# Rounding weights to FP4 beside an attention: |q| on ScalarE, a maximum on VectorE, scales for two chunks at once, four buffers

## What is computed

```python
def fp4_quant_dequant(x):                        # blocks of 16 along the last dim
    scale = jnp.max(jnp.abs(xb), axis=-1, keepdims=True) / 6.0
    scale = jnp.maximum(scale, jnp.float32(1e-12))
    xn = xb / scale
    idx = jnp.searchsorted(_MID, jnp.abs(xn))    # _MID  0.25 0.75 1.25 1.75 2.5 3.5 5
    q = _GRID[idx] * jnp.sign(xn) * scale        # _GRID 0 .5 1 1.5 2 3 4 6

def fp4_linear(x, w):
    xq, wq = fp4_quant_dequant(x), fp4_quant_dequant(w)
    return jnp.einsum('bsk,nk->bsn', xq, wq)

gate, y = fp4_linear(x, w_gate), fp4_linear(x, w_up)      # w: 1408 x 512
h = jax.nn.silu(gate) * y
out = fp4_linear(h, w_down)
```

## Time and profile before

| | |
|---|---|
| median of 3 runs (lowest to highest) | 1689.22 us (1686.55 to 1689.85) |
| the profiled execution | 1689.68 us, its span 1687.9 us |
| busy in the span | PE 1471.6 (87%), PEld 1060.0 (63%), DVE 773.1 (46%), ACT 466.4 (28%), POOL 557.9 (33%) |
| the rounding of the gate and up weights | 227 to 341 us |
| the block that holds it | ends at 347.2 us, the next one starts at 348.4 us |

### The profile page before, as it was taken

How to read it: one execution, slowest core, us unless ns; L and a number is a source line. 1 busy time by engine, 2 the same in 40 slices (tenths; PEclk the granted TensorE clock), 3 DMA queues, 4 the chain that set the end, 5 groups by cost and what they waited for, 6 DMA issues and landing times. The chain is left out here.

```text
span 1687.9 us, 26535 instructions
## 1 busy us (share of the span) xinstructions
PE 1471.6 (87%) x11120; PEld 1060.0 (63%) x11120; DVE 773.1 (46%) x1333; ACT 466.4 (28%) x772; POOL 557.9 (33%) x315
## 2 busy tenths in 40 slices
PE   8788977477988999999999999999998896936796
PEld 3556755243444778778787787788776673415573
DVE  2455279989435341332322323222232315978913
ACT  0323301031111115243242433324243431303302
POOL 6102057656323032122122122231232324617701
PEclk9779975788998999999999999999999998967997
DMA  5300030010101411111111111111012016003000
GB/s 233 149 1 1 0 137 1 0 69 0 75 0 64 147 51 57 52 34 53 39 42 51 39 48 42 38 52 57 30 42 78 22 57 256 0 0 119 1 0 25
DMA packets 50101, 91.29 MB, mean 54 GB/s; under 512 B 28600, under 2 KB 41664, under 8 KB 46912
## 3 DMA queue, kind: packets, MB, share of 16 engines
q1 hardware_dynamic: 49984, 89.60, 15.1%
HBM read 79.89 MB, written 9.70 MB: 53 GB/s over the span
## 5 line engine op out<-in xcount | busy, mean ns | idle before, releaser
L1074 POOL TENSOR_TENSOR ctx_hi<-ctx_raw,one 128x1536 fp32r<-128x1536 f32 (+1 forms) x36 | 102.9, 2858 | 617.5 <-DMA ctx_raw<-in_ctx 426.0
L1328 DVE TENSOR_TENSOR V<-PS,vbias 128x512 f32<-128x512 f32 (+1 forms) x104 | 71.9, 691 | 338.0 <-PE PS L1114 337.8
L1256 ACT COPY ET<-PS 128x512 f32<-128x512 f32 (+1 forms) x224 | 129.6, 585 | 299.1 <-PE PS L1170 295.4
L1359 DVE TENSOR_SCALAR_CACHE_REDUCE E<-PS 128x384 f32<-128x384 f32 (+1 forms) x256 | 131.8, 571 | 159.6 <-PE PS L1147 159.0
L1170 PE MATMUL PS<-ident,E 128*128 128x128 f32 (+1 forms) x832 | 127.3, 278 | 8.8 <-ACT ET L1256 8.8
L1077 POOL TENSOR_TENSOR ctx_raw_r<-ctx_raw,ctx_hi 128x1536 fp32r<-128x1536 f32 (+1 forms) x36 | 131.2, 3644 | 2.8
L1114 PE MATMUL PS<-ctx_raw_r,wk_hi 128*128 128x384 f32 (+1 forms) x512 | 128.6, 355 | 0.0
L1114 PE MATMUL PS<-wv_lo,ctx_hi 128*128 128x512 f32 (+1 forms) x416 | 125.9, 405 | 0.0
L1114 PE MATMUL PS<-ctx_hi,wk_hi 128*128 128x384 f32 (+1 forms) x512 | 122.9, 361 | 2.5 <-POOL ctx_raw_r L1077 2.5
L1263 ACT ACTIVATE E<-E,peak 128x1601 f32<-128x1601 f32 x64 | 103.5, 1623 | 64.8 <-DVE peak L1364 64.8
L1114 PE MATMUL PS<-wv_hi,ctx_hi 128*128 128x512 f32 (+1 forms) x416 | 120.5, 411 | 0.8 <-issue 0.8
(11 more groups left out here) (283 smaller groups left out, 2383.3 us busy)
## 6 DMA issues: line engine op xcount, KB each, us to landing
ctx_raw<-in_ctx SPq DMA_DIRECT2D x27, 768.0 KB, 4.4
ctx_raw<-in_ctx_first SPq DMA_DIRECT2D x9, 900.0 KB, 4.6
rel_scr<-rel_out SPq DMA_DIRECT2D x8, 640.0 KB, 3.8
fwk<-in_fwk SPq DMA_DIRECT2D x1, 4096.0 KB, 25.4
fwv<-in_fwv SPq DMA_DIRECT2D x1, 4096.0 KB, 12.7
corr<-rel_scr SPq DMA_DIRECT2D x64, 48.0 KB
p_scr<-E SPq DMA_DIRECT2D x16, 192.0 KB, 2.3
near<-p_scr SPq DMA_DIRECT2D x64, 48.0 KB
```

Of the source, the lines that this page charges most:

```text
L1074: nc.gpsimd.tensor_tensor(ctx_hi[r][:, :, 0:n], ctx_raw[r][:, :, 0:n], one[:].unsqueeze(1).broadcast_to([P, KC, n]), ALU.mult).then_inc(S[ ...
L1256: nc.scalar.copy(ET[0:n, j % ET_RING, :], src[0:n, :]).then_inc(S["et_out"], 1)
L1328: v.tensor_tensor(V[0:rows, at % V_RING, :], bank(4 + NUMBER[unit] % 2)[0:rows, :], vbias[0:rows, :], ALU.add).then_inc(S["v_out"], 1)
L1359: v.tensor_scalar(E[:, p, k0:k0 + n], bank(r)[:, 0:n], 1.0, None, ALU.mult, ALU.max, accum_out=tops[:, p, c:c + 1]).then_inc(S["s_out"], 1)
```

## The change

`WeightRounding` no longer uses `Fp4` (which `fp4_layer` still does). It works in pairs of chunks. VectorE takes two block maxima, and makes scale, reciprocal and factor for both in one instruction each, of 88 numbers per partition. ScalarE makes |q| times GRID = 2^22 + 1 (`scalar`), VectorE takes the maximum of that and GRID (`floor`) for the pair before, and GpSimd adds and subtracts that number as before. Mask (L581) and magic number (L582) are gone. GpSimd joins chunks 0 to 7, VectorE 8 to 15 (`join_by_vector`). q and grid have four buffers, the scales three pairs. ScalarE's 16 instructions are placed in the attention's program: two after each copy of the context, two after the exponential of t = 2 and t = 3 and in the same place at the last tile, two at the end.

```diff
@@ small_attention, vector
                 other(2)
+            if beside:
+                beside.finish(dve)
@@ small_attention, scalar
             for t in range(NT):
                 if t + 1 < NT:
                     exponentials(t + 1)
+                if beside and t >= 1:
+                    beside.scalar(act, 2)
                 act.wait_ge(pt_ps, t + 1)
...
                 act.wait_ge(o_ps, t + 1)
                 nc.scalar.copy(oT[...]).then_inc(o_out, 1)
+                if beside:
+                    beside.scalar(act, 2)
+            if beside:
+                beside.scalar(act, 2)
@@ WeightRounding
-    BY_POOL = CHUNKS - 5
+    BY_POOL = CHUNKS // 2
+    STAGES = 4
+    GRID = 2.0 ** 22 + 1.0
...
     def vector(self, dve, ch, count):
-        for n in range(self.started, min(self.started + count, self.CHUNKS)):
-            if n % (self.CHUNKS // 2) == 0:
-                dve.wait_ge(self.s.loaded["wg" if n == 0 else "wu"], 16)
-            self.fp4.divide(dve, ch, n, self.chunk(n))
-            self.started = n + 1
-            for k in range(self.CHUNKS):
-                if k >= self.BY_POOL and (k + 2 == n or (n == self.CHUNKS - 1 and k + 2 > n)):
-                    self.fp4.join(dve, self.nc.vector, k, self.chunk(k))
+        v = self.nc.vector
+        for n in range(self.started, min(self.started + count, self.CHUNKS), 2):
...
+            if n >= 2 * len(self.scale):
+                for k in range(2):
+                    self.wait_joined(dve, n + k - 2 * len(self.scale))
+            for k in range(2):
+                ch.add(v.tensor_reduce(self.scale_of(n + k), self.chunk(n + k), AX.X, ALU.max, apply_absolute_value=True))
+            ch.sync()
+            sc, inv = self.scale[n // 2 % len(self.scale)][:], self.inverse[:]
+            ch.link(v.tensor_scalar(sc, sc, float(np.float32(1 / 6)), 1e-12, ALU.mult, ALU.max))
+            ch.link(v.reciprocal(inv, sc))
+            ch.link(v.tensor_scalar(inv, inv, 1.0 - 2.0 ** -23, None, ALU.mult))
+            self.floor(dve, n)
+            self.join_by_vector(dve, n - 2)
+            for k in range(2):
+                if n + k >= self.STAGES:
+                    self.wait_joined(dve, n + k - self.STAGES)
+                v.tensor_tensor(blocks(self.q[(n + k) % self.STAGES][:]), self.chunk(n + k),
+                                inv[:, k].unsqueeze(2).broadcast_to([P, self.WIDTH // BLOCK, BLOCK]), ALU.mult).then_inc(self.divided, 1)
+            self.started = n + 2
+
+    def floor(self, dve, end):
+        for n in range(self.floored, end):
+            grid = self.grid[n % self.STAGES][:]
+            dve.wait_ge(self.sized, n + 1)
+            self.nc.vector.tensor_scalar(grid, grid, self.GRID, None, ALU.max).then_inc(self.ready, 1)
+        self.floored = max(self.floored, end)
+
+    def join_by_vector(self, dve, end):
+        for n in range(self.joined, end):
+            dve.wait_ge(self.rounded, 2 * n + 2)
+            self.join(self.nc.vector, n).then_inc(self.joined_dve, 1)
+        self.joined = max(self.joined, end)
+
+    def finish(self, dve):
+        self.floor(dve, self.CHUNKS)
+        self.join_by_vector(dve, self.CHUNKS)
+
+    def scalar(self, act, count):
+        for n in range(self.measured, min(self.measured + count, self.CHUNKS)):
+            act.wait_ge(self.divided, n + 1)
+            self.nc.scalar.activation(self.grid[n % self.STAGES][:], self.q[n % self.STAGES][:], ACT.Abs,
+                                      scale=self.GRID).then_inc(self.sized, 1)
+            self.measured = n + 1
...
     def pool(self, pool):
         for n in range(self.CHUNKS):
-            self.fp4.round(pool, n, self.WIDTH)
+            q, grid = self.q[n % self.STAGES][:], self.grid[n % self.STAGES][:]
+            pool.wait_ge(self.ready, n + 1)
+            self.nc.gpsimd.tensor_tensor(q, q, grid, ALU.add).then_inc(self.rounded, 1)
+            pool.wait_ge(self.rounded, 2 * n + 1)
+            self.nc.gpsimd.tensor_tensor(q, q, grid, ALU.subtract).then_inc(self.rounded, 1)
             if n < self.BY_POOL:
-                self.fp4.join(pool, self.nc.gpsimd, n, self.chunk(n))
+                pool.wait_ge(self.rounded, 2 * n + 2)
+                self.join(self.nc.gpsimd, n).then_inc(self.done, 1)
```

More of the change, by code:

```diff
@@ L608 @@
     CHUNKS = 2 * IC * D // WIDTH
-    BY_POOL = CHUNKS - 5
+    BY_POOL = CHUNKS // 2
+    STAGES = 4
+    GRID = 2.0 ** 22 + 1.0
     def __init__(self, nc, sem, region, s):
-        self.nc, self.s, self.fp4, self.started = nc, s, Fp4(nc, sem, region, "fp4w", self.WIDTH, 3), 0
+        self.nc, self.s, self.started, self.measured, self.floored, self.joined = nc, s, 0, 0, 0, self.BY_POOL
+        nb = self.WIDTH // BLOCK
+        self.q = [region.tensor(f"fp4w_q{r}", [P, self.WIDTH]) for r in range(self.STAGES)]
+        self.grid = [region.tensor(f"fp4w_grid{r}", [P, self.WIDTH]) for r in range(self.STAGES)]
+        self.scale = [region.tensor(f"fp4w_scale{r}", [P, 2, nb]) for r in range(self.STAGES // 2 + 1)]
+        self.inverse = region.tensor("fp4w_inverse", [P, 2, nb])
+        self.divided, self.sized, self.ready, self.rounded, self.done = (
+            sem("fp4w_" + n) for n in ("divided", "sized", "ready", "rounded", "done"))
+        self.joined_dve = sem("fp4w_joined_dve")
     def chunk(self, n):
@@ L617, in chunk, with scale_of, wait_joined @@
         return blocks(w[:, n * self.WIDTH:(n + 1) * self.WIDTH])
+    def scale_of(self, n):
+        return self.scale[n // 2 % len(self.scale)][:, n % 2]
+    def wait_joined(self, eng, n):
+        if n < self.BY_POOL:
+            eng.wait_ge(self.done, n + 1)
+        else:
+            eng.wait_ge(self.joined_dve, n - self.BY_POOL + 1)
     def vector(self, dve, ch, count):
-        for n in range(self.started, min(self.started + count, self.CHUNKS)):
+        v = self.nc.vector
+        for n in range(self.started, min(self.started + count, self.CHUNKS), 2):
@@ L631, in pool, with join @@
+    def join(self, ops, n):
+        return ops.tensor_tensor(self.chunk(n), blocks(self.q[n % self.STAGES][:]),
+                                 self.scale_of(n).unsqueeze(2).broadcast_to([P, self.WIDTH // BLOCK, BLOCK]), ALU.mult)
     def pool(self, pool):
         for n in range(self.CHUNKS):
-            self.fp4.round(pool, n, self.WIDTH)
+            q, grid = self.q[n % self.STAGES][:], self.grid[n % self.STAGES][:]
[3 more added lines that the diff above has]
+            self.nc.gpsimd.tensor_tensor(q, q, grid, ALU.subtract).then_inc(self.rounded, 1)
```

## The result

The changed kernel takes 1678.11 us (median of 4 runs, 1674.96 to 1680.29) against 1689.45 us; the ratio is 0.9934, 95% interval 0.9919 to 0.9949. It is faster by 0.7%, 11.3 us, where 7.7 us were forecast; the time lies inside the stated range. The profiled execution took 1677.72 us, its span 1675.9 us.

What follows compares the result with a forecast made beforehand. VectorE was taken to bound the edited block. Its stretches sum to 119.1 us against 128.0; with 1.1 us added for the layout's shortfall, it ends 7.7 us earlier: 1689.22 becomes 1681.5 us, range 1676 to 1688.5.

Steps and rivals of the forecast that it cites:

- What bounds: Second small attention, rounding of gate and up weights: VectorE limits the block; its gains move everything behind one for one.
- The turns: In the rounding, VectorE's port-using instructions and GpSimd's exclude each other and alternate; a VectorE product costs 2.27 us per turn.
- A removed instruction gives back its own part: VectorE in the rounding: removal saves the instruction's own time; its wait moves to the next one needing a turn.
- The count of 28 us: Rival counting VectorE's removed time alone, waits shrinking with the instructions: 28 us saved, 1661 us; chance 0.08 with anything near.
- The stretches: Block laid out from weigh(t) to weigh(t+1) for t=0 to 3, then the end: sum 119.1 us against 128.0.
- The second maximum: Second pair at t=0: VectorE's second maximum of |q| and GRID comes behind GpSimd's add, 2.1 us.
- |q| on ScalarE: 16 instructions of 0.76 us each; GpSimd's first add waits behind the context copy until 235.2, costing VectorE nothing.
- rival (3): Slower: ScalarE reloads its function table between Exp and Abs, five times in the block; 1686 or 1691 us; chance 0.06.
- near 340: Sign of a right forecast: the second small attention block ends near 340 us instead of 347.
- the blocks behind shift as a whole; I allow 1 us either way: Blocks after the changed one move by its gain, with 1 us allowed either way.

Runs made afterwards that it cites:

- without GpSimd's turns: GpSimd's three instructions a chunk cut to 16 of 704 numbers, in both kernels: stretch 87.94 us before, 78.03 after; single executions of 1659.21 and 1646.11 us.
- the mask: Changed kernel with exponent mask and magic number back on VectorE, ScalarE making nothing: stretch 121.05 us for 112.40; kernel 1690.66 us, ratio 1.0004 to the kernel before.
- the scales: Changed kernel with scale, reciprocal and factor made for each chunk by itself: stretch 117.50 us for 112.40; kernel 1685.53 us, ratio 0.9987 to the kernel before.
- The second comparison: Changed kernel, unedited, run again beside the kernel before on another run's chip: stretch 112.35 us; kernel 1681.05 us over 7 runs for 1688.79, ratio 0.9954.

## Why the prediction was right, and where its size was off

- **What bounds.** VectorE, and a quarter of the old stretch is its waiting for turns. Shown: without GpSimd's turns VectorE's busy time falls from 112.06 to 81.47 us, and the old stretch from 119.95 to 87.94.
- **The turns.** A product 2.27 us from turn to turn: two divisions took 4.66, a join 2.17 on average. A removed instruction gives back its own part: shown by the mask (8.7 us for instructions of 8.4 us) and the scales (5.1 us for 4.1 and their gaps). The joins don't follow it: two fewer on VectorE gave 3.0 us for 1.8 of their own, eight fewer cost 0.7, because those turns go to GpSimd. The count of 28 us was wrong for the reason given; the 20 us by which the divisions grew and the 10 of the joins ate it.
- **The stretches.** 22.2, 25, 26.4, 30 and 15.6 us plus 1.1 were laid out; 21.52, 26.43, 26.42, 30.03 and 16.46 were measured. The second is 1.4 off: the softmax product met a running GpSimd instruction there too, 2.50 us for 1.22, which I had charged to the third stretch alone. The row, which is the same again in the third stretch:

```profile
240.16 2.50 DVE L381 TENSOR_TENSOR XT<-XN,a_sm 128x1024 f32<-128x1024 f32 x1
```

  The second maximum, which I had behind GpSimd's add in the first stretch, got its turn ahead of it, and both divisions waited instead. That was one turn fewer: maxima and divisions took 5.6 us where 6.9 were laid out. A longer wait for the scores, 8.5 us until the first block maximum for 8.0, took some of it back. The prediction's addition is off too. The parts as it lists them, rounded as they are, make 22.35, 25.3, 26.7, 30.1 and 15.6, together 120.1 and not 119.1, so they give 6.8 us and not 7.7.
- **|q| on ScalarE.** 0.79 us for an estimated 0.76; GpSimd's first add at 233.63 in a block that began some 1.7 us earlier, so 235.3 on the old clock for 235.2. The wait that it adds to VectorE is 0.4 us, once. The reloads of rival (3) didn't come: the first table load behind the start of the span is still that of the SiLU in the next block:

```profile
356.23 1.28 ACT L854 ACT_TABLE_LOAD   x1
```

  Here "ScalarE: Activation LUTs" of the Trainium skill, section "Table sets: the hidden batching unit", which lists abs in the set of exp, is borne out: 16 Abs among the Exp without a load.
- **The block as a whole** got shorter by 7.1 us over the stretches as I laid them out (128.0 to 120.86), and by 7.55 from the first block maximum on, where I had 7.7. It ends at 337.97 us, 339.6 on the old clock, where "near 340" was expected. That it comes so close is partly luck: the turn too many in the first stretch and the product missed in the second, 1.3 us each, cancel.
- **The step that failed** is "the blocks behind shift as a whole; I allow 1 us either way". What lies outside the stretch was 4.5 us shorter in the profiled execution (1563.50 for 1567.95), 1.7 of it ahead of the change. Over 14 profiled executions it moved by 6 us with the same work in it, so a single comparison can carry 3 to 4 us that aren't the change's. The second comparison gave 7.7 us, the stretch's own gain: its median is 2.9 us above the first, and its profiled execution took 1340.83 us behind the stretch for the 1340.71 of the kernel before. The changed kernel's two values for the outside, 1563.50 and 1564.05, are still the lowest of the fourteen. The second is low by its part ahead of the change (223.22), which the change can't have shortened. So nothing here shows that any of the 11.3 us beyond the 7.55 belongs to the change, and a share of 1 to 3 us is not excluded. What sets TensorE's time for the same matmuls in the last blocks no run separated; its granted clock there is 0.85 in both rows.

## What to carry over

- When two engines exclude each other at a port, read an instruction's duration as work plus waiting, and price an edit by laying the new order out in turns. An instruction taken away gave back its own work here (mask, scales); the wait moves to the next one that needs the port.
- Then order matters as well as count. An instruction that needs no port costs nothing between two that do (4.65 us with it, 4.66 without), though only part of that reached the end: 3.0 us for moving 14 block maxima. Moving work to the other engine pays only while that one runs dry: of 8, 10 and 16 joins on GpSimd, 10 was best.
- Judge such a change by the stretch that it touches, where two executions agree to 0.05 us, and only then by the whole, where they don't agree to 3 (two executions of one code, 1565.46 and 1568.39 us outside the stretch).

## What the runs showed of the hardware

- VectorE and GpSimd take turns one instruction each. In the changed kernel's block 28 of VectorE's instructions and 34 of GpSimd's that use the port were held by more than 0.1 us, taking the shortest of each form as its own time, and neither engine got two in a row while the other waited; nor did it in the block of any other trace kept here. The two divisions in 4.66 us are one such place. "SBUF — State Buffer" of the Trainium skill, section "Who interferes with whom", calls the shared ports an exclusive lock that is held for the whole instruction, and the traces agree: the division issued at 248.77 waits out GpSimd's add until 250.39.
- A tensor_scalar of 88 numbers per partition waits for a running GpSimd instruction to its end just as one of 704 does: 1.54 us (L660, a row of the changed kernel's timeline, below) for 0.21, behind GpSimd's instruction that ends at 258.06. Making two of them one brought little beyond their own time all the same: 24 small instructions fewer, 4.1 us by their own times, brought 5.1 us.

```profile
256.59 1.54 DVE L660 TENSOR_SCALAR fp4w_scale<-fp4w_scale 128x88 f32<-128x88 f32 x1
```
